# Post-norm transformer chain on one core: one score tile moved ahead of the softmax transposes, weight pieces re-ordered

## The reference

```
L0 attention: scores = einsum('bci,bcj->bij', x, x)      # 256 x 256 per batch, summed over tokens
              weights = softmax(scores); context = einsum('bij,bcj->bci', weights, x)
L0 MLP:       W = table[4-bit codes] * block scales      # gate, up: 2048 x 256, down: 256 x 2048
              out = (gelu(x Wg^T) * (x Wu^T)) Wd^T
L1 attention: a Mamba-2 state-space block (projection, convolution, chunked scan, gate, projection)
L1 MLP:       silu(x W1) * (x W2), two of every four kept, then W3
```

## Time and profile before

| what | value |
|---|---|
| median of three runs | 1228.03 us (1227.83 to 1228.88) |
| the profiled execution, its own time | 1228.34 us |
| its span in the profile | 1226.5 us |
| TensorE's mean granted clock | 0.991 of full |
| PE busy | 1189.2 us, 97% |
| VectorE (DVE) busy | 826.0 us, 67% |
| ScalarE (ACT) busy | 615.1 us, 50% |
| GpSimd (POOL) busy | 420.4 us, 34% |

### The profile page before, as it was taken

One profiled execution on the slowest core, in us unless ns is written; L12 is line 12 of the kernel. 1 busy time (PEld: TensorE's weight loads), 2 busy tenths in 40 slices (PEclk: granted clock), 3 DMA queues, 4 the chain that ended last, 5 costly groups with the idle time before them and its releaser, 6 DMA issues.

```text
span 1226.5 us, 20808 instructions
## 1 busy us (share of the span) xinstructions
PE 1189.2 (97%) x7168; PEld 1019.8 (83%) x7168; DVE 826.0 (67%) x1550; ACT 615.1 (50%) x1242; POOL 420.4 (34%) x561
## 2 busy tenths in 40 slices
PE   6899999999999999999999999999999999999996
PEld 6788888888888888888877788887877788888886
DVE  5787635445353544534469888888875999898998
ACT  4444323233332323333458998989885554444441
POOL 1203100000000000000047888888884434444434
PEclk8999999999999999999999999999999999999998
DMA  5222100101010010100001011110111000111101
GB/s 206 88 68 91 35 1 1 35 1 35 1 35 1 2 32 0 52 0 18 1 13 35 28 53 52 51 30 21 51 52 35 27 16 20 34 34 34 34 18 35
DMA packets 31113, 42.21 MB, mean 34 GB/s; under 512 B 2576, under 2 KB 23056, under 8 KB 30928
## 3 DMA queue, kind: packets, MB, share of 16 engines
q1 hardware_dynamic: 31056, 41.45, 10.5%
HBM read 27.94 MB, written 12.58 MB: 33 GB/s over the span
## 4 chain that ended last, share of the span: by engine, by line
PE 87%; DVE 7%; ACT 3%; issue 2%; POOL 0%; DMA 0%; POOLq 0%; DVEq 0%; ACTq 0%; SPq 0%; PEldq 0%
PE bank L48 26%; PE bank L50 24%; PE bank L49 24%; PE bank L1996 2%; PE bank L1977 2%; PE bank L1987 1%; PE bank L1959 1%; PE bank L1923 1%; DVE beats L1567 1%; PE bank L1967 1%; DVE dab L1584 1%; PE bank L1878 1%; PE bank L1730 1%; PE bank L1879 1%; DVE dh L1551 1%
## 5 line engine op out<-in xcount | busy, mean ns | idle before, releaser
L1274 DVE TENSOR_TENSOR hb<-gl,bank 128x512 f32<-128x512 f32 x128 | 87.9, 687 | 202.3 <-PE bank L50 197.3
L793 ACT ACTIVATE hh<-hb 128x512 fp32r<-128x512 f32 x128 | 80.9, 632 | 185.1 <-DVE hb L1274 185.1
L838 ACT ACTIVATE gl<-bank 128x512 f32<-128x512 f32 x128 | 76.7, 599 | 184.9 <-PE bank L50 184.9
L1237 DVE TENSOR_TENSOR hl<-hb,hh 128x512 fp32r<-128x512 f32 x128 | 93.7, 732 | 78.9 <-ACT hh L793 78.9
L771 POOL TENSOR_TENSOR dhl<-dab,dhh 128x512 fp32r<-128x512 f32 x63 | 95.4, 1536 | 126.7 <-ACT dhh L793 126.6
L580 POOL TENSOR_TENSOR veb<-mvb,eps 128x4 f32<-128x4 f32 x8 | 1.6, 201 | 317.5 <-DVE mvb L1254 317.5
L48 PE MATMUL bank<-xt_l,w_h 128*128 128x512 f32 x256 | 102.7, 401 | 1.0 <-DVE dh L1551 0.5
L48 PE MATMUL bank<-at_l,w_hi_a 128*128 128x512 f32 x256 | 102.8, 402 | 0.6 <-PE bank L50 0.3
L50 PE MATMUL bank<-at_h,w_hi_b 128*128 128x512 f32 x256 | 101.4, 396 | 0.0
L50 PE MATMUL bank<-at_h,w_hi_a 128*128 128x512 f32 x256 | 101.3, 396 | 0.0
L48 PE MATMUL bank<-at_l,w_hi_b 128*128 128x512 f32 x256 | 101.3, 396 | 0.0
(11 more groups left out here) (256 smaller groups left out, 3565.1 us busy)
## 6 DMA issues: line engine op xcount, KB each, us to landing
xg<-x_scratch SPq DMA_DIRECT2D x16, 512.0 KB, 3.9
xg<-in_xt SPq DMA_DIRECT2D x8, 512.0 KB, 4.8
x_scratch<-rows_out SPq DMA_DIRECT2D x8, 512.0 KB, 3.1
x_scratch<-rows_out SPq DMA_DIRECT2D x16, 256.0 KB, 2.2
xall<-in_x SPq DMA_DIRECT2D x7, 512.0 KB, 8.9
out<-rows_out SPq DMA_DIRECT2D x7, 512.0 KB, 3.2
wq<-in_codes SPq DMA_DIRECT2D x12, 256.0 KB, 2.7
sc<-in_scales SPq DMA_DIRECT2D x12, 256.0 KB, 3.0
```

What stands on the lines that cost most here:

```text
L793: return act.activation(dst, src, ACT.Copy)
L838: act.activation(gl[:, n % 2], ps_gate[n % 2][:], ACT.Gelu_apprx_tanh).then_inc(s_gelu, 1)
L1237: return dve.tensor_tensor(dst, src, hi.bitcast(F32), ALU.subtract)
L1274: dve.tensor_tensor(hb[:, n % 2], gl[:, n % 2], ps_up[n % 2][:], ALU.mult).then_inc(s_h, 1)
```

## The change

On PE, `scores(4)` (batch 1's first tile) goes ahead of `softmax_transpose(0)`, and `scores(6)` ahead of `x1_transpose(0)`. ScalarE and VectorE make the halves of x for these tiles earlier to match. On VectorE, piece 0's two parts are parted by xs_low(3); piece 1's are put around `ln1_apply(0)`, behind `ln1_stats(0)`; piece 2's around `score_max(1)`. On GpSimd, `inv_std(0)` comes ahead of the low half of piece 1. Piece 3 is made inside MLP group 0, in round 0 (its bits behind that round's hl), its low half now on VectorE, and the table of the pieces 4 to 11 is moved with it: pieces 7, 8, 9, 10 and 11 come later by one or two rounds. No operation is added or removed.

```diff
-        DEQUANT_AT = {0: 4, 1: 5, 3: 6, 4: 7, 6: 8, 8: 9, 9: 10, 10: 11}
+        DEQUANT_AT = {0: 3, 1: 4, 3: 5, 4: 6, 6: 7, 7: 8, 9: 9, 10: 10, 11: 11}
...
-            for j in range(2):
-                weights_lo(j)
+            weights_lo(0)
             inv_std(0, mv, ve, rstd, s_ln1, s_ln1r)
-            for j in range(2, 4):
+            for j in range(1, 3):
                 weights_lo(j)
             inv_std(1, mv, ve, rstd, s_ln1, s_ln1r)
...
             xs_hi_first()
-            for f in range(1, GPB):
+            for f in range(1, GPB + 1):
                 xs_hi(f)
             weights_hi(0)
             score_exp(0)
             x_hi(0)
             softmax_hi(0)
-            xs_hi(GPB)
             xs_hi(GPB + 1)
+            xs_hi(GPB + 2)
             act.wait_ge(c_small, 96)
             act.activation(a4[:], a4[:], ACT.Exp).then_inc(c_a4, 1)
-            weights_hi(1)
-            xs_hi(GPB + 2)
             xs_hi(GPB + 3)
             for k in range(KT):
                 a_hi(0, k)
+            weights_hi(1)
+            score_exp(1)
             weights_hi(2)
-            score_exp(1)
-            weights_hi(3)
...
-                    if isinstance(g, int) and g == 0 and n in DEQUANT_AT:
+                    if isinstance(g, int) and g == 0 and n > 0 and n in DEQUANT_AT:
                         dequant_bits(DEQUANT_AT[n])
                     h_lo(g, n)
 
+                    if isinstance(g, int) and g == 0 and n == 0:
+                        dequant_bits(DEQUANT_AT[n])
...
             xs_low_first()
-            for f in range(1, GPB):
+            for f in range(1, GPB - 1):
                 xs_low(f)
-            dequant(0)
+            dequant_bits(0)
+            xs_low(GPB - 1)
+            dequant_scale(0)
+            xs_low(GPB)
             score_max(0)
             softmax_scale(0)
             x_lo(0)
             softmax_lo(0)
-            xs_low(GPB)
             xs_low(GPB + 1)
-            dequant(1)
+            xs_low(GPB + 2)
             ln1_stats(0)
-            xs_low(GPB + 2)
+            dequant_bits(1)
             ln1_apply(0)
+            dequant_scale(1)
             xs_low(GPB + 3)
             for k in range(KT):
                 a_lo(0, k)
-            dequant(2)
+            dequant_bits(2)
             score_max(1)
-            dequant(3)
+            dequant_scale(2)
...
             for f in range(GPB):
                 scores(f)
+            scores(GPB)
             softmax_transpose(0)
             context(0, 0)
-            scores(GPB)
             scores(GPB + 1)
+            scores(GPB + 2)
             x1_transpose(0)
-            scores(GPB + 2)
             scores(GPB + 3)
```

More of the change, by code:

```diff
@@ L1195, in weights_low @@
                                       ALU.subtract).then_inc(s_wlo, 1)
-            def dequant(j):
-                dequant_bits(j)
-                dequant_scale(j)
             dve.wait_ge(s_const, 11)
```

## The result

| | before | after |
|---|---|---|
| median (runs) | 1228.32 us (20) | 1230.32 us (20) |
| ratio after / before, undisturbed runs | | 1.0017, 95% interval 1.0011 to 1.0023 |
| the profiled execution, its own time | 1228.34 us | 1231.81 us |

The account below looks back on a forecast made before the run. TensorE, busy 97% of 1226.5 us, was taken as the bound, so only its pauses and slow clock could yield. Nearly all of the 7.4 us front lead was to be lost again: 1228.34 - 1.05 = 1227.3, range 1224.5 to 1230.2.

Parts of the forecast that it names:

- The front: Start through first down projection: context at full clock, gate(0) 5.8 us earlier, down(0) 7.4 us earlier, at 46.4.
- port term: Front: piece 2's bits on VectorE collide with GpSimd's low half of piece 1; 1.2 us, bounds 0 and 2.5.
- Group 0, up to up(12): MLP group 0: late low halves of pieces 7 and 10 cause pauses of 1.8 and 2.1 us; lead falls to 3.6.
- Lead of this event: 1.0 us: End of group 0: the last low half (piece 11) ends at 105.3 against 106.27 before, only 1.0 us earlier.
- rival B: Before batch 1's softmax transposes: the new 3.2 us pause lets the clock fall, costing 1.6 us; 1228.9, chance 0.27.
- Moved by 1.0 at the start: GpSimd's conversions of the state-space weights start 1.0 us earlier than 112.69, following the last low half.
- The wall: Group 1, round 0: VectorE's hl and softmax_scale(1) wait on GpSimd's win_l and wo_l; TensorE stands from 124.0 to 127.2.
- 3.2 us pause: TensorE's wait near 125, before batch 1's softmax transposes, takes nearly the whole gain; no slow clock included in the forecast sum.
- The sum: At down(1, 0): 128.5 against 129.59 before, so -1.05 us for the whole kernel, giving 1227.3.
- A: The forecast itself: lead eaten by the piece order and then by the VectorE-GpSimd port, 1227.3; chance 0.40.

Follow-up runs that it names:

- e7: Changed kernel with GpSimd's conversions of the state-space weights held until batch 1's softmax transposes are done: 1223.79 us, ratio 0.9966.
- e8: Changed kernel with pieces 7, 9, 10 and 11 a round earlier and GpSimd's win_l and wo_l split into parts: 1221.18 us, ratio 0.9945.
- e12: Changed kernel with idle transposes filling two pauses, 24 ahead of batch 1's softmax transposes and 20 between gate(12) and up(12): 1229.56 us, ratio 1.0011.
- e3: Changed kernel with GpSimd's win_l split into eight instructions and wo_l into four: 1223.19 us, ratio 0.9960.
- e1: Changed kernel with 24 transposes of a constant put ahead of batch 1's softmax transposes: 1229.04 us, ratio 1.0006.
- e6: Changed kernel with pieces 7, 9, 10 and 11 made a round earlier in the table: 1222.90 us, ratio 0.9959.
- e4: Changed kernel's front order alone, with piece 3 back in the front and the old round table: 1226.36 us, ratio 0.9987.
- e2: Changed kernel with batch 1's softmax scaling, transposes and halves one round later in group 1: 1226.74 us, ratio 0.9987.
- e9: Kernel before, old front order, with only piece 3 moved into group 0 and the changed kernel's round table: 1234.21 us, ratio 1.0045.
- e5: Kernel before with GpSimd's win_l split into eight instructions and wo_l into four: 1226.55 us, ratio 0.9989.
- e10: Changed kernel with pieces 7, 9, 10 and 11 a round earlier and GpSimd's conversions held until batch 1's softmax transposes: 1221.58 us, ratio 0.9948.
- e11: Changed kernel with the earlier piece table, split GpSimd conversions and batch 1's softmax steps one round later: 1220.67 us, ratio 0.9938.

## Why the prediction was wrong, point by point

- **The front.** Right, nearly to the digit. The x1 transposes, forecast at 33.6, come at 34.15 in this late-starting execution; gate(0), forecast at 39.1, comes at 39.82 here and at 39.16 and 39.19 in the traces of e7 and e8, which share the front; down(0), forecast at 46.4, comes there at 46.36 and 46.40. The context runs at full clock. Piece 2's bits took 2.08 instead of the 0.76 of two free ones, 1.3 more, where the port term said 1.2.
- **Group 0, up to up(12).** Right: pauses of 1.64 and 2.02 where 1.8 and 2.1 stood, both ended by the low halves of pieces 7 and 10.
- **"Lead of this event: 1.0 us".** Failed: the last low half ended 0.5 us later than before, at 106.77, not 105.3. Of the 1.5 us, 0.6 is the late start of this execution, 0.5 the slow clock behind up(12) (e12); 0.4 is left over. I had put the pause of 2.1 into the sum and not the clock behind it, though rival B had that very mechanism for the next pause. The same omission is in TensorE's lead: 3.6 forecast, 1.2 measured at down(12), of which the slow clock took 1.6 and the late start 0.6.
- **"Moved by 1.0 at the start".** Failed further: the same 512 KB of wo_raw took 7.0 us instead of 5.9, so GpSimd started 1.6 later instead of 1.0 earlier. It was taken at its old duration, without a bound. It is no accident of one trace: all seven kernels with the changed kernel's table took 6.8 to 7.9 us for it (last section), so the median execution may have met the wall later still.
- **The wall.** The mechanism was right: the pause is there, ended by the softmax rows, and e3 and e7 show it by taking it away. That it measured 3.23 where 3.2 was forecast is in part luck. TensorE was to stand from 124.0 to 127.2 and stood from 125.9 to 129.15: its arrival, for the want of the clock term, and the wall, for the two steps above, were both 1.9 us later than forecast, and the difference of the two stayed. The rule of the Trainium skill's page "SBUF — State Buffer", section "Who interferes with whom", on which this leaned, agrees with these rows: 2.94 us for an hl that met win_l whole, 1.18 for one that met an eighth of it.
- **"3.2 us pause", clock.** Failed: I gave rival B, in which the clock falls, a chance of 0.27, and it came. Its price was short, too: 1.6 against 2.65 in this trace (1.3 in the medians of e1). By the Trainium skill's page "TensorE: Matmul & The Clock Gate", Part 1, the throttled clock is the default that activity releases. e1 agrees (filled pause, no slow stretch behind it), and so does e12 in its first filled pause, but behind its second one the clock fell all the same.
- **The sum.** -1.05 forecast for down(1, 0), +0.88 measured: 1.5 from the last low half, 1.1 from the weights, less 0.7 that GpSimd's own chain and rows_out took less than I had put. With 2.65 for the clock: 1227.3 + 1.9 + 2.65 = 1231.9, and the profiled execution took 1231.81; the slow stretch in the state-space block is in both profiled executions and drops out of this sum. So it was B's mechanism behind A's, from a later wall. By the medians the change costs 2.0: an estimate from the same terms, without the late start of 0.6 and that stretch of 1.2, is 1230.0, against 1230.32 measured.
- **Why the gain of 6.7 us in the front gave nothing.** It was not lost, only blocked: with the conversions split it comes out as 1223.19, with the held ones 1223.79, with the better table 1222.90.

Left open: 0.4 us of the last low half's delay, why wo_raw took longer (below), and why the clock's cost is 2.65 in the changed kernel's trace but 1.3 between the medians (0.6 of it is that e1's wall came later, 131.04 against 130.47, as its wo_raw took 7.8 us). Besides the two kernels' own tables only that of e6 was tried.

## What to carry to other kernels

Time won at the front is kept only if every producer that the later stages wait for moves forward too: here the table of due rounds was moved back while TensorE was moved forward, and four entries of it decided 7.4 us. Look in particular for one long instruction on an engine that shares a port with the critical producer; cut it into parts, or hold it back until the critical step is past, and cost each predicted pause of TensorE with the slow clock behind it.

## What the runs showed of the hardware that was not expected

- **The clock falls behind shorter pauses than the 3.0 us of before, and not behind every pause of one length.** In the first 140 us, single pauses of 1.36, 1.50 and 1.64 to 1.65 us (the last before up(8), in every trace with the changed kernel's table) had no slow stretch of their own. Those of 1.75 (e4), 1.79 (e6), 2.02 and 2.03 (before up(12), in every trace with that table but e12's, where it was filled), 2.26 (e2) and 3.23 each had one. In e12 a wait of 1.64 behind filling transposes, followed by 0.66 of work and more waiting, had one from 132 to 135 as well, while e1's 1.33 in the same place had none. Further on the length does not decide: behind the pause of 1.19 at 644.60 the changed kernel's trace has a slow stretch, and e1's has none behind the same pause at 642.43; near the end of the program a pause of 2.26 to 2.28 had one in the changed kernel's trace (1215 to 1218, behind 1213.54) and none in those of e9 and e12. What else decides was not found.
- **The same transfer lands at different times.** From its issue, the load of wo_raw took 5.9 us in the kernel before and in e5, 6.0 to 6.5 in the kernels with the old or with e6's table (e4, e6, e8, e10, e11), and 6.8 to 7.9 in all seven with the changed kernel's table (e7 6.8, the changed kernel 7.0, e12 7.2, e9 7.6, e2 7.7, e1 7.8, e3 7.9). In the changed kernel the first microseconds move less (in the window 108 to 109: 361 GB/s before, 213 after, the issue 0.5 apart), but in e7 they do not (416, its issue 0.2 earlier than before). What sets it was not found.
- **TensorE at the start.** From 6.8 to 10.0 us the changed kernel's score matmuls are 0.21 us apart although the windows show a granted clock of 1.00; in e12 this lasts until 12.5. Its window from 10 to 12 us:

```profile
10.00:12.00 2.00, 2.00 (x11) 2.00 (x11) 0.00 (x0) 0.00 (x0) 0.00 (x0) 1.00 1.06 393
```

  Whether the clock's record begins too late or the 16 busy DMA engines slow the operands is open. e12's context starts 0.7 us later than the changed kernel's (26.17 against 25.47); the other 0.75 of its 1.48 came from GpSimd's two steps of `inv_std(0)`, which took 0.63 and 1.47 us instead of 0.29 and 1.07. Over all traces with the new front order the context starts between 24.80 (e7) and 26.17 (e12), so a start late in a trace is to be taken off before two traces are compared.
